# Six value-projection matmuls of layer 1 moved from the last two pairs of layer 0 in between the next batch's query projections

## What is computed

```python
# layer 0
q = x @ Wq + bq;  k = ctx @ Wk + bk;  v = ctx @ Wv + bv
attn = softmax(q k^T * scale + mask);  x = layernorm((attn v) @ Wo + bo + x)
# layer 1
a = layernorm(ctx)
Q = x @ Wq.T;  K = a @ Wk.T;  V = a @ Wv.T
x = x + tanh(gate) * ((softmax(Q K^T * scale) V) @ Wo.T)
```

## Time and profile before

| | |
|---|---|
| median of 3 runs | 1238.1 us (1238.07 to 1238.13) |
| the profiled execution | 1238.88 us, span of its instructions 1237.1 us |
| TensorE busy | 1163.7 us, 94% of the span |
| DVE, ACT, POOL busy | 810.3, 749.9 and 259.9 us |
| mean granted TensorE clock | 0.991 of full speed |

### The profile page before, as it was taken

How to read it: one execution, slowest core, us unless ns; L and a number is a source line. 1 busy time by engine, 2 the same in 40 slices (tenths; PEclk the granted TensorE clock), 3 DMA queues, 4 the chain that set the end, 5 groups by cost and what they waited for, 6 DMA issues and landing times.

```text
span 1237.1 us, 32215 instructions
## 1 busy us (share of the span) xinstructions
PE 1163.7 (94%) x9987; PEld 942.3 (76%) x9987; DVE 810.3 (65%) x2387; ACT 749.9 (61%) x2163; POOL 259.9 (21%) x280
## 2 busy tenths in 40 slices
PE   4899999999999999999999999999999999999997
PEld 4678787777878777787877778777787877778785
DVE  4465667667576775757667575766757576676734
ACT  3374756747475674747567474856747476574744
POOL 2042213121131312113121121312112131212210
PEclk9799999999999999999999999999999999999999
DMA  7674536447353654736365472635637263563600
GB/s 240 180 175 99 143 88 157 117 100 189 81 156 76 147 134 91 193 75 156 86 135 146 88 195 68 163 88 123 158 88 181 71 162 98 110 167 81 149 11 8
DMA packets 77821, 153.77 MB, mean 124 GB/s; under 512 B 10384, under 2 KB 47056, under 8 KB 77152
## 3 DMA queue, kind: packets, MB, share of 16 engines
q1 hardware_dynamic: 77792, 153.40, 50.6%
HBM read 113.72 MB, written 39.65 MB: 124 GB/s over the span
## 4 chain that ended last, share of the span: by engine, by line
PE 72%; issue 12%; DVE 9%; ACT 4%; DMA 1%; DVEq 1%; POOL 1%; ACTq 0%; SPq 0%; POOLq 0%
PE PJ L365 17%; PE TP L416 13%; PE SCO L402 6%; PE OA L436 5%; PE SCO L460 5%; PE SCO L681 5%; PE PJ L378 5%; PE PJ L468 4%; DVE SCO L819 3%; PE SCO L406 3%; PE SCO L365 2%; ACT PR L1049 2%; DVE PT L829 2%; DVE MN L819 1%; PE SCO L666 1%
## 5 line engine op out<-in xcount | busy, mean ns | idle before, releaser
L1049 ACT ACTIVATE PR<-SCO,MN 100x361 f32<-100x361 f32 x768 | 424.8, 564 | 154.3 <-DVE MN L819 151.1
L819 DVE CUSTOM_DVE_ANT_0 SCO<-SCO,MK 100x361 f32<-100x361 f32 x768 | 402.3, 549 | 148.1 <-PE SCO L402 102.3
L416 PE MATMUL TP<-ident,PR 100*128 100x100 f32 x2304 | 268.4, 252 | 22.3 <-DVE PT L829 19.7
L416 PEld LDWEIGHTS TP<-ident,PR 100*128 100x128 f32 x2304 | 226.9, 141 | 80.5 <-DVE PT L829 27.1
L1060 ACT ACTIVATE PT<-TP 121x600 f32<-121x600 f32 x256 | 173.0, 676 | 77.0 <-PE TP L416 76.6
L402 PE MATMUL SCO<-K0S,Q0S 128*100 128x362 f32 x512 | 164.1, 375 | 19.7 <-ACT PR L1049 17.5
L1049 ACT ACTIVATION_READ_ACCUMULATOR PR<-SCO,MN 100x1 f32 x768 | 158.2, 206 | 0.0
L829 DVE COPY PT<-TP 121x600 f32<-121x600 f32 x128 | 100.0, 781 | 52.1 <-PE TP L416 50.1
L819 DVE DVE_READ_ACCUMULATOR2_ANT MN<- 100x1 f32 x768 | 108.7, 141 | 0.0
L402 PEld LDWEIGHTS SCO<-K0S,Q0S 128*100 128x100 f32 x512 | 75.4, 166 | 43.1 <-ACT PR L1049 38.2
L406 PE MATMUL SCO<-K1S,Q1S 128*100 128x362 f32 x256 | 96.6, 387 | 8.1 <-ACT Q1S L1171 5.0
(11 more groups left out here) (142 smaller groups left out, 1827.7 us busy)
## 6 DMA issues: line engine op xcount, KB each, us to landing
K1S<-k_scr SPq DMA_DIRECT2D x128, 364.0 KB, 6.1
k_scr<-K1HL SPq DMA_DIRECT2D x64, 364.0 KB, 2.5
Q0S<-q_scr SPq DMA_DIRECT2D x128, 100.0 KB, 3.9
K0S<-k_scr SPq DMA_DIRECT2D x64, 182.0 KB, 4.8
AT<-ctx_cols SPq DMA_DIRECT2D x16, 722.0 KB, 9.3
V<-ctx_rows SPq DMA_DIRECT2D x16, 484.0 KB
q_scr<-QHL SPq DMA_DIRECT2D x16, 400.0 KB, 2.5
k_scr<-K1HL SPq DMA_DIRECT2D x32, 182.0 KB, 3.1
```

Source lines behind the costliest of these rows:

```text
L416: last = pe.transpose(TP[:, k % 2, c * T:(c + 1) * T], PR[0:T, k % NPR, c * SP:c * SP + P], ident[0:T, 0:T])
L819: dve.tensor_tensor_reduce(out=bank, in0=bank, in1=mask[0:T, :], scale=scale, scalar=3.4e38, op0=ALU.add, op1=ALU.min, accum_out=MN[0:T, k ...
L1049: act.activation(PR[0:T, k % NPR, 0:S], SCO[0:T, k % 3, 0:S], ACT.Exp, bias=MN[0:T, k:k + 1], scale=-1.0, accum_out=SM[0:T, k:k + 1]).then ...
```

## The change

The pairs 14 and 15 keep 2 and 0 value steps instead of 5 and 3 (batch 0: 0 and 0 instead of 4 and 2). The six steps 30 to 35 stand between the steps of `queries0`: three among the first four, three among the next six. In the last batch they take the place of ten repeated keys. No instruction of another engine is changed, and no wait.

```diff
-        V1_STEPS = spans({3: 4, 5: 3, 6: 5, 10: 5, 11: 5, 12: 1, 13: 5, 14: 5, 15: 3})
+        V1_STEPS = spans({3: 4, 5: 3, 6: 5, 10: 5, 11: 5, 12: 1, 13: 5, 14: 2})
-        FIRST_V1_STEPS = spans({9: 6, 10: 6, 11: 6, 12: 6, 13: 6, 14: 4, 15: 2})
+        FIRST_V1_STEPS = spans({9: 6, 10: 6, 11: 6, 12: 6, 13: 6})
                 if more:
                     pe.wait_ge(l_xt, 16 * b + 32)
                     pe.wait_ge(v1_ev, 3 * b + 2)
-                    queries0(range(4))
+                    for i in range(3):
+                        queries0((i,))
+                        values1(b, (30 + i,))
+                    queries0((3,))
                 else:
                     pe.wait_ge(v1_ev, 3 * b + 2)
-                    repeated_keys(4)
+                    values1(b, range(30, 33))
                 transpose_probs(b, 14)
                 if more:
-                    queries0(range(4, 10))
+                    for i in range(3):
+                        queries0((2 * i + 4,))
+                        values1(b, (33 + i,))
+                        queries0((2 * i + 5,))
                 else:
-                    repeated_keys(6)
+                    values1(b, range(33, 36))
                 transpose_probs(b, 15)
```

## The result

The changed kernel takes 1273.5 us in the median (1271.97 to 1275.88, 6 runs), against 1238.1 us for the kernel before measured with it. The ratio is 1.028, with a 95% interval from 1.0268 to 1.0292. It is slower by 35.4 us. The forecast was 1273.0.

A forecast was written before the change was run, and what follows sets the result against it. TensorE's own work was taken as the bound. Per batch 2.29 us plus 0.04 make 2.33; 15 x 2.33 - 0.1 = 34.9 us turns the 1238.1 us median into 1273.0, own range 1269 to 1277, full range 1258 to 1280.

The forecast's parts named there:

- What bounds the kernel: Whole batch period: TensorE's own work sets the time, busy 69.92 of 72.77 us, with 2.85 us idle per batch.
- What is taken away: Pairs 14 and 15: 1.37 us of work leaves, but pair 13's transposes stay at 457.54, so nothing is gained.
- What they cost in the new place: Tail, among the query steps: TensorE has almost no gap, so the six steps add 1.37 us per batch.
- the mixture: Tail: changing from fp32 to fp32r matmuls costs 0 to 0.12 us for six changes, taken as 0.04.
- Faster: Tail: interleaved query records go at the transposes' pace, 0.08 us instead of 0.111, saving 5.4 us in all; chance 0.03.
- What is late next: Tail, first `keys0` step: DVE gets step 35 late, so TensorE waits 0.92 us for the splits.
- The chain: DVE, from the start of the cast to the end of the last subtraction: 4.15 us.
- The sum: Per batch 2.29 us plus 0.04, so 2.33; 15 x 2.33 - 0.1 = 34.9 us in all.
- A hidden chain: First `keys0` step: DVE's new wait does not show and only 1.37 us a batch remain, 1258.6 us; chance 0.05.
- ACT did not run ahead: Pairs 14 and 15: rival that earlier scores pull ACT forward, leaving 0.92 us a batch, 1252 us; chance 0.05.
- absorbed: TensorE's idle 2.85 us a batch: rival that it swallows 2.29 us of delay, time stays at 1238; chance 0.04.
- the clock: Each batch: rival of 14 us at the lower level, adding 105 us; chance 0.05, shared with another late engine.

The follow-up runs named there:

- the half moves: Kernel before with three value steps of pair 15, or in a twin three of pair 14, moved behind the first three query steps: 1248.6 and 1248.0 us.
- the kernel with the splits first: Changed kernel with DVE's repeated sums and two splits put ahead of its wait for step 35 and the cast, TensorE's program unchanged: 1259.7 us.
- the block: Changed kernel with the six value steps as one block ahead of the query steps instead of between them: 1259.5 us.

## Why the prediction was right, step by step

- *What bounds the kernel.* TensorE's work sets the time outside the pairs where ACT does. The first is shown by the six steps, which cost their length in the tail, the second by the run without them, and the half moves show it for each pair.
- *What is taken away.* The transposes of pair 13 were to start 0.05 us behind ACT's copy with about 0.7 us idle before them, and 0.4 ahead of the second score. They do, with 0.70. The score's wait is given as 0.22, but from the start of the first score to that of the second it is 468.49 - 467.88 = 0.61 us, some 0.4 more than the 0.2 between them before. The wait of 0.1 us or more ahead of the transposes of pair 12 is there too: 467.37 - 466.98 = 0.39 us behind the start of step 29, which takes 0.23.
- *What they cost in the new place.* 1.37 us and 0.04 for the mixture were predicted. The kernel with DVE's wait out of the way has a period 74.10 - 72.77 = 1.33 us longer. The two terms together were put 0.08 us too high. The mixture costs nothing or less, and that 0.04 came near it is luck: the two records ahead of the value step in the earlier trace rows are L453's and not a query step's, and were given the query records' 0.111 us. At the 0.08 us of the transposes, which have as many columns, the three would take 2 x 0.08 + 0.228 = 0.39 at their own paces, so the 0.47 show a loss of 0.08 a change, or 0.5 us for six. It is there, and query records that run faster give it back, as the last section shows. The rival *Faster* had such a gain in it, but not the loss.
- *What is late next.* The cast was to start 463.55 - 457.54 = 6.01 us behind the transposes of pair 13. It starts 475.68 - 469.59 = 6.09 behind them. The chain was to take 4.15 and takes 4.16. The predicted wait of 0.92 us stands against 0.82 in the row, which counts from a modelled end. By starts the first `keys0` step comes 479.89 - 478.68 = 1.21 us behind L453, where it was 0.17: 1.04 us of delay, 0.12 more than predicted. Not all of it lasts. From `out0` to the next transposes of pair 13 it was 530.31 - 466.58 = 63.73 us and is 544.62 - 481.00 = 63.62, so 0.11 us come back there, where the prediction had every engine follow as before. Most of that lies within `out0`: to the `keys0` step behind it, it was 3.35 us and is 3.26. Before, `out0` waited for `unit_outputs` in each batch (2.9 us in 16 waits in the whole span), which the prediction took to come just in time. In the changed kernel one such wait of 0.2 us is left. What the wait is worth is 75.04 - 74.10 = 0.94 us a period, by the run that takes it away and leaves TensorE's program as it is.
- *The sum.* 2.33 us a batch were predicted, and 2.27 measured. The spans of the profiled executions differ by 34.8 us, against 34.9 predicted, and part of that agreement is luck. From the first query step in the tail of batch 14 to the end of the span it is 1271.9 - 1146.8 = 125.1 us after and 1237.1 - 1114.3 = 122.8 before. That is 2.3 us more, one period's growth in full, so the 0.1 us that the last batch was to give back do not show. And 0.7 us of the 34.8 come from before the first batch's query steps (93.4 against 92.7 us). That point moves by more than 0.7 us between executions: the kernel with the splits first, with the same program on TensorE, has it at 91.8. Without the 0.7 it is 15 x 2.27 = 34.1 us.
- *The rivals.* A hidden chain (1258.6 us) is what the block and the new DVE order turn the kernel into, at 1259.5 and 1259.7. So that price was right, and the condition was not met. ACT did not run ahead, no more than 0.1 us a batch was absorbed, and the clock stayed at its full level in the windows of the batches (1.00), with 0.990 as the mean of the span against 0.991.

## What to carry to other kernels

A matmul that covers a wait is free, and moving it to a place where TensorE is busy costs its whole length. Whether it is free is read from the other engine, here ACT's rows without a gap, and not from the idle time beside it, which is small just because the cover works. Ask of the last moved instruction who waits for its semaphore and what stands behind that wait in the queue: here 40% of the loss (0.94 of 2.27 us) was a wait on DVE that had never been felt. And a wait that vanishes from the list of waits is a gain only if the period of the loop gets shorter.

## What was not expected of the hardware

Query records between value steps start faster one behind the other than among themselves. In the kernel after, a value step and the two records of the query step behind it take 472.10 - 471.65 = 0.45 us together, the same as 2 x 0.111 + 0.228 = 0.45 at their own paces, though the value step itself then spans 0.31 us rather than 0.23 (471.65 to 471.96). So the fp32r matmul behind an fp32 one takes 0.08 us more to the next start, and the two query records behind it take 472.10 - 471.96 = 0.14 us instead of 0.22 and give that back. In the group of the earlier trace rows the value step also takes 0.30 us to the next start, but L453's records ahead of it take their usual 0.17, the same as ahead of `keys0` in the earlier trace rows, and give nothing back. The Trainium skill, TensorE: Matmul & The Clock Gate, section "Step-by-step: what each phase is for", says that weights are loaded while a matmul runs, which fits records that are short behind a long matmul. What share of the 0.08 us is due to it no run here separates.
